# Cross attention whose transposed scores are computed a second time, with the maxima in a contraction row

## The chip, the cores and the metric

The kernel runs on one core of one Trainium2 chip. The metric is the device time of one execution in microseconds (us), lower is better. It is a decoder layer with batch 8, 112 tokens per batch and width 256: self attention, cross attention over 375 context tokens, and an expert layer, each followed by a layer norm. All arithmetic is float32.

## The reference, cut to what matters

Only the cross attention is touched. It has 16 heads of 16 columns each. In this case the scale is 1/4, and the mask has one row pattern for all batches and heads.

```python
q = _split_heads(query @ Wq.T + bq)      # (8, 16, 112, 16)
k = _split_heads(key @ Wk.T + bk)        # (8, 16, 375, 16)
v = _split_heads(value @ Wv.T + bv)
scale = 1.0 / jnp.sqrt(jnp.float32(HEAD_DIM))
scores = jnp.einsum('bhqd,bhkd->bhqk', q, k) * scale
scores = jnp.where(mask == 0, NEG_INF, scores)
probs = jax.nn.softmax(scores, axis=-1)
out = jnp.einsum('bhqk,bhkd->bhqd', probs, v)
out = out.transpose(0, 2, 1, 3).reshape(query.shape[0], -1, D_MODEL)
return out @ Wo.T + bo
```

## The kernel before, in words

Every engine has its own hand-written list of instructions, and semaphores join them. Nothing is scheduled by a tool: an instruction that waits holds back all that stands behind it on its engine.

**Slots.** Cross attention runs in 32 slots (`SLOTS`), n = 0 to 31. A slot handles four heads of one batch: b = n // 4 is the batch, g = n % 4 the group of heads. The four heads of a slot lie in four strips of 32 partitions (`STRIPS`), since a head has 16 columns and two heads share a strip; queries of the other head of the strip are zeroed in `qz`, so a contraction over 32 rows gives one head's scores.

**One slot before.** TensorE (PE) computes the scores of four heads, queries as weights (`score2`, L617), each 112x375 into its own PSUM bank. VectorE (DVE) reads each, adds the mask, writes the sum to `p2` and keeps its row extreme in `nm2` (`mask_and_max`, L1232; signs are turned, so the maximum is a minimum). ScalarE (ACT) takes the exponential from `p2` with that extreme as its bias (`exps2`, L996). PE transposes each 112x375 block of probabilities in three pieces of 125 columns (`turn2_`, L635, 12 transposes in a slot), and ACT (three heads, `evac_pt`, L1003) and DVE (one head, `evac_pt2`, L1240) copy the result from PSUM to `pT2`. PE multiplies with the values (`value2`, L651); a column of ones in `v2` gives the softmax sums.

**What stands between.** PE's list for slot n is: `score2(n)`, two transposes groups of slot n-1, a filler, the other two groups, more fillers, `value2(n-2)`. The fillers are the projections of the next batch's keys (`project_k`, L526) and values (`project_v`, L532), of queries for every second batch (`project_q`, L518), the transposes of the output (`turn_o`, `turn_on`), the output projection (`out2`, L670) and the transposes for the next layer (`turn_x2`). Keys go to SBUF on ACT (`evac_k`, L951), values with their bias on DVE (`evac_v`, L1181), the attention output of a batch on DVE (`evac_ot`, L1246), and DVE also does the division (`normalise2`), the second layer norm (`ln2_a`, `ln2_b`) and the query scaling (`evac_q`, L1174).

**Around it.** Self attention comes before, with its own loop over the 8 batches; DVE scales the queries' mask factor at the end of its batch 1 (`query_scale`), and `out1` (L504) is its output projection. After the slots PE runs the shared expert (`shared`, L790, `shared_down`, L801), while the router's decisions are made on DVE, GpSimd (POOL) scatters the tokens by indirect DMA (L384), and the sorted tiles are loaded back (L294) and transposed (`head_tile`, L848) for the loop over expert tiles.

## Time and profile before

| | |
|---|---|
| time, median of 3 runs | 438.22 us (438.16 to 438.72) |
| profiled execution | 438.09 us, its span 436.3 us |
| PE busy | 413.4 us, 95% of the span |
| DVE busy | 243.3 us, 56% |
| ACT busy | 193.8 us, 44% |
| POOL busy | 51.0 us, 12% |
| granted TensorE clock, mean | 0.996 of 2.4 GHz |

The span is what the profiler sees between the first and the last instruction; 1.8 us of the profiled execution lie around it. Busy shares are means over stages with different limits: self attention takes the first 165 us, the 32 slots lie between 164.7 and about 329 us, the shared expert and the routing up to 366 us, and the loop over expert tiles the rest. In the rows, PEld is the loading of weights, L617 a line of the kernel, and a bracket says how long the engine stood idle before the instruction and who released it.

### The profile page before, as it was taken

To read this page: it belongs to the slowest core of one execution; us is meant where nothing else is said; L and a number is where in the kernel's file an instruction comes from. 1 tells how busy PE (TensorE), PEld (TensorE's weight loads), DVE (VectorE), ACT (ScalarE), POOL (GpSimd) and SP (SyncE) were. 2 spreads that over 40 slices of the span, in tenths; PEclk is the share of its full clock that TensorE was granted. 3 is DMA by queue.
4 is the path that set the end of the run, shared out by engine and by line. 5 is a ranking of instruction groups with operands and counts; after the bars stand their busy time and mean duration, and the time that the engine had idled before them with its cause. 6 is when DMAs were issued, how large, how long until landed. Compare 5 with 4: busy or idle time off the path is not lost.

```text
span 436.3 us, 8960 instructions
## 1 busy us (share of the span) xinstructions
PE 413.4 (95%) x3125; PEld 296.9 (68%) x3126; DVE 243.3 (56%) x724; ACT 193.8 (44%) x580; POOL 51.0 (12%) x77
## 2 busy tenths in 40 slices
PE   8999999999999988999999999999989998999992
PEld 7767879778796765766776676767665474656661
DVE  1275765747556546666665676767762552244442
ACT  1164363343625536677666666767663101111110
POOL 4010010110101001000010101010100045212222
PEclk9999999999999999999999999999999999999998
DMA  8998000000000014040404131900000013122211
GB/s 248 373 382 236 19 2 2 0 2 2 1 2 0 2 37 145 2 181 16 167 16 167 52 131 46 390 37 2 2 2 2 1 50 108 49 62 69 62 42 33
DMA packets 15242, 34.22 MB, mean 78 GB/s; under 512 B 2382, under 2 KB 9151, under 8 KB 13921
## 3 DMA queue, kind: packets, MB, share of 16 engines
q1 hardware_dynamic: 13952, 30.70, 20.3%
q0 software_dynamic: 1104, 2.76, 1.8%
q8 instruction: 25, 0.41, 0.4%
q10 hardware_dynamic: 144, 0.23, 0.2%
q14 instruction: 17, 0.13, 0.1%
HBM read 27.24 MB, written 6.70 MB: 78 GB/s over the span
## 4 chain that ended last, share of the span: by engine, by line
PE 68%; issue 23%; DVE 4%; ACT 1%; SPq 1%; DMA 0%; POOLq 0%; POOL 0%; DVEq 0%; ACTq 0%
PE bank L434 11%; PE bank L635 7%; PE bank L448 7%; PE bank L504 6%; PE bank L617 4%; PE bank L880 4%; PE bank L856 4%; PE bank L532 3%; PE bank L862 3%; PE bank L465 3%; PE bank L491 3%; PE bank L526 3%; PE bank L651 3%; PE bank L477 3%; PE bank L801 1%
## 5 line engine op out<-in xcount | busy, mean ns | idle before, releaser
L1232 DVE CUSTOM_DVE_ANT_0 p<-bank,mask 112x375 f32<-112x375 f32 x128 | 62.7, 546 | 39.2 <-PE bank L617 39.2
L996 ACT ACTIVATE p<-p,nm 112x375 f32<-112x375 f32 x128 | 74.8, 609 | 5.9 <-DVE nm L1232 5.9
L635 PEld LDWEIGHTS bank<-ident,p 112*125 112x125 f32 x384 | 48.9, 187 | 22.8 <-issue 13.7
L1003 ACT ACTIVATE pT<-bank 125x336 f32<-125x336 f32 x96 | 42.9, 447 | 46.0 <-PE bank L635 46.0
L635 PE MATMUL bank<-ident,p 112*125 112x112 f32 x384 | 58.8, 286 | 0.9
L434 PE MATMUL bank<-x2T,arena 128*128 128x224 f32 x256 | 53.9, 359 | 0.0
L939 ACT ACTIVATE p<-bank,nm 112x112 f32<-112x112 f32 x128 | 43.6, 366 | 18.3 <-DVE nm L1106 18.3
L434 PEld LDWEIGHTS bank<-x2T,arena 128*128 128x128 f32 x256 | 47.3, 193 | 0.7 <-DMA x2T<-in_xT 0.6
L349 POOL TENSOR_TENSOR rstd<-veps,minus_half 128x1 f32<-128x1 f32 x14 | 7.7, 549 | 292.6 <-DVE veps L1132 292.6
L1106 DVE TENSOR_REDUCE nm<-bank 112x4 f32<-112x448 f32 x32 | 19.2, 620 | 24.1 <-PE bank L465 24.1
L1099 DVE TENSOR_SCALAR arena<-bank 128x448 f32<-128x448 f32 x32 | 19.9, 623 | 22.0 <-PE bank L434 22.0
L617 PE MATMUL bank<-kT,qz 32*112 32x375 f32 x256 | 28.8, 517 | 3.5 <-ACT x2T L965 2.1
L448 PE MATMUL bank<-arena,x2T 128*112 128x512 f32 x64 | 30.2, 602 | 0.0
L945 ACT ACTIVATE arena<-bank 128x448 f32<-128x448 f32 x16 | 8.7, 544 | 46.8 <-PE bank L491 46.8
L939 ACT ACTIVATION_READ_ACCUMULATOR p<-bank,nm 112x1 f32 x128 | 28.1, 220 | 0.0
L504 PE MATMUL bank<-arena 128*128 128x256 f32 x112 | 26.0, 385 | 1.4 <-ACT arena L945 1.0
L532 PE MATMUL bank<-wx,mid 128*125 128x256 f32 x96 | 26.5, 399 | 0.0
L790 PE MATMUL bank<-x2T,ugs 128*128 128x512 f32 (+1 forms) x64 | 25.5, 543 | 0.6 <-DVE pT L1313 0.4
L651 PE MATMUL bank<-pT,v 125*32 125x112 f32 x768 | 25.0, 263 | 0.0
L1073 ACT ACTIVATE p<-bank 128x512 f32<-128x512 f32 x9 | 5.4, 597 | 44.0 <-PE bank L856 44.0
L651 PEld LDWEIGHTS bank<-pT,v 125*32 125x32 f32 x768 | 17.3, 109 | 10.1 <-issue 7.4
L504 PEld LDWEIGHTS bank<-arena 128*128 128x128 f32 x112 | 20.7, 190 | 4.8 <-ACT arena L945 1.3
(140 smaller groups left out, 596.2 us busy)
## 6 DMA issues: line engine op xcount, KB each, us to landing
arena<-in_ug SPq DMA_DIRECT2D x8, 1024.0 KB, 5.8
arena<-in_dn SPq DMA_DIRECT2D x8, 512.0 KB, 6.7
mid<-in_ctxT SPq DMA_DIRECT2D x8, 375.0 KB, 3.1
slots_s<-blank SPq DMA_DIRECT2D x14, 128.5 KB, 3.6
arena<-in_wqk SPq DMA_DIRECT2D x7, 256.0 KB, 5.7
slots_x<-blank SPq DMA_DIRECT2D x14, 128.0 KB, 6.6
p<-slots_s SPq DMA_DIRECT2D x9, 128.5 KB, 2.0
kT<-slots_x SPq DMA_DIRECT2D x9, 128.0 KB
```

The costliest lines, as they stand in the source:

```text
L434: mm = pe.matmul(J[:, m * S_PAIR:(m + 1) * S_PAIR], wqk[:, 2 * u + m, k, :], xT[:, i, k, :], start=(k == 0), stop=(k == KC - 1))
L448: mm = pe.matmul(PE_J1[c][0:S, :], xT[:, b // 2, k, (b % 2) * S:(b % 2 + 1) * S], wv1[:, c, k, :], start=(k == 0), stop=(k == KC - 1))
L504: mm = pe.matmul(PE_W1[:, 0:C], oT1[:, k, t * TILE:(t + 1) * TILE], wout[:, k, :], start=(k == 0), stop=(k == 7))
L532: mm = pe.matmul(M[0:SK, 0:C], ctxT[:, b % 2, k, t * SK:(t + 1) * SK], wx[:, 2, k, :], start=(k == 0), stop=(k == KC - 1))
L617: mm = pe.matmul(PE_S2[r][0:S, 0:S2], qz[rows_r, b // 2 % 2, m, par, b % 2, :], kT2[rows_r, b % 2, m, :], start=True, stop=True)
L635: mm = pe.transpose(PE_T2[r][0:SK, t * S:(t + 1) * S], p2[i % RING][:, t * SK:(t + 1) * SK], ident[0:S, 0:S])
L651: mm = pe.matmul(PE_V2[VP * r:VP * r + VP, g * S:(g + 1) * S], v2[:, b % 2, t, g * STRIPS + r, :], pT2[0:SK, (n * STRIPS + r) % RING, t, : ...
L790: mm = pe.matmul(bank[2 + 2 * (n % 2) + part][:, 0:width(grp)], ugs[:, k, part * HID + m * 128:part * HID + (m + 1) * 128], x2T[:, k, grp ...
L939: e = act.activation(p1[g][:, n, :], PE_S1[g % 2][0:S, n * S:(n + 1) * S], ACT.Exp, bias=nm1[:, h:h + 1], accum_out=rs1[:, h:h + 1])
L996: act.activation(p2[i % RING], p2[i % RING], ACT.Exp, bias=nm2[:, i % H:i % H + 1], scale=-1.0).then_inc(exp2, 1)
L1003: act.activation(pT2[0:SK, i % RING], PE_T2[r][0:SK, 0:KT * S].rearrange("p (k n) -> p k n", k=KT), ACT.Copy).then_inc(pt2_act, 1)
L1232: v.tensor_tensor_reduce(p2[i % RING], PE_S2[r][0:S, 0:S2], bias[:], 1.0, 3e38, ALU.add, ALU.min, accum_out=nm2[:, i % H:i % H + 1]).then_ ...
```

## The change

The probabilities are no longer transposed. Instead the scores are computed a second time in transposed form, with the keys as weights, and the exponential is taken from that.

- A contraction of 32 rows has 16 rows that belong to the strip's other head, and they multiply zeros. `kx` now holds the keys twice, once for each parity of head, and in one of these rows (the pole) it holds -1. `mask_and_max` writes its extreme into the column of `nmx` that belongs to this row; PE transposes `nmx` (`turn_nm`), and DVE adds the transposed rows to the slot's queries (`add_nm`), which gives `qm`. The second product `kx` by `qm` (`score2_turned`) then is the score minus its maximum, already transposed: 3 pieces by 4 heads, each 125x112.
- ACT takes the exponential straight from PSUM to `pT2`, 125x336 for a head, with no bias.
- The mask isn't in the second product, so masked entries are set to zero after the exponential, with the transposed mask `maskT`: POOL does one head of a slot in two instructions (minimum with 1, then product), DVE three heads in one minimum over 125x1008 (`keep_unmasked`).
- Keys are written by ACT and DVE, half of the columns each, twice (for each parity). The value bias is folded into the output bias `rows[:, 1]` by a product in self attention's batch 1, and values and attention outputs are now copied by ACT (`evac_v2`, `evac_o2`).
- PSUM is shared differently: banks 0 to 3 hold the scores, banks 4 to 7 the transposed ones, and fillers borrow from both, so each waits for the mask or the exponential that frees its bank.
- `out1` of the last tile moves into slot 0, the projection of keys for batch 1 into self attention's last batch, `turn_x1(2)` out of it. Three pieces of the shared expert, in place of one, stand before the router's last transposes. `kx` lies over the weights of expert 0, so its load waits for the last `score2_turned`.

The core of the diff:

```diff
+        kx = arena[:, 0:4 * KC * S2].rearrange("p (b m a n) -> p b m a n", b=2, m=KC, a=2)
@@ sync
+            for j, e in enumerate(range(1, E)):
+                load_expert(e)
+                if j + 3 < B:
+                    load_ctx(j + 3)
+            sp.wait_ge(turned2, SLOTS)
+            load_expert(0)
@@ gpsimd
+            def keep_unmasked(n):
+                i = n * STRIPS
+                g.wait_ge(exp2, i + 1)
+                p = pT2[0:SK, i % RING].rearrange("p k n -> p (k n)")
+                g.tensor_scalar(p, p, 1.0, None, ALU.min).then_inc(at_most_one, 1)
+                g.wait_ge(at_most_one, n + 1)
+                g.tensor_tensor(p, p, maskT[0:SK, :], ALU.mult).then_inc(kept_pool, 1)
@@ tensor
+                    for k in range(KC):
+                        mm = pe.matmul(PE_W1[:, C:2 * C], bvw[:, k, :], wx[:, 3, k, :], start=(k == 0), stop=(k == KC - 1))
+                    mm.then_inc(bo_more, 1)
...
-            def turn2_(n, r):
-                for t in range(KT):
-                    mm = pe.transpose(PE_T2[r][0:SK, t * S:(t + 1) * S], p2[i % RING][:, t * SK:(t + 1) * SK], ident[0:S, 0:S])
+            def turn_nm(n):
+                pe.wait_ge(max2, (n + 1) * STRIPS)
+                pe.transpose(PE_N2, nmx[:, n % GROUPS, :], ident[0:S, 0:S]).then_inc(nm_pe, 1)
+            def score2_turned(n):
+                pe.wait_ge(qm_sb, n + 1)
+                lent_banks_back(n)
...
+                    pe.wait_ge(exp2, n * STRIPS)
+                for t in range(KT):
+                    for r in range(STRIPS):
+                        rows_r = slice(32 * r, 32 * r + 32)
+                        mm = pe.matmul(PE_T2[r][0:SK, t * S:(t + 1) * S], kx[rows_r, b % 2, m, par, t * SK:(t + 1) * SK],
+                                       qm[rows_r, n % 2, :], start=True, stop=True)
+            def fillers(n):
+                first_free(n)
...
+                elif g < 2 and b + 1 < B:
+                    pe.wait_ge(max2, n * STRIPS + 2)
+                    project_k(g, b + 1, [(PE_S2[0], 0, KH), (PE_S2[1], KH, S2)])
...
+                turn_nm(n)
...
+            for n in range(SLOTS):
+                score2(n)
+                if n >= 1:
+                    score2_turned(n - 1)
+                if n >= 2:
+                    value2(n - 2)
+                fillers(n)
@@ scalar
+            for n in range(SLOTS):
+                if n >= 1:
+                    exps2(n - 1, 0)
+                if n >= 2:
+                    evac_o2(n - 2)
+                if n >= 1:
+                    exps2(n - 1, 1)
+                first_out(n)
+                if n >= 1:
+                    exps2(n - 1, 2)
+                    exps2(n - 1, 3)
+                lent_out(n)
@@ vector
+            def keep_unmasked(n):
+                i = n * STRIPS + 1
+                v.wait_ge(exp2, i + 3)
+                p = pT2[0:SK, i % RING:i % RING + 3].rearrange("p r k n -> p r (k n)")
+                v.tensor_tensor(p, p, maskT[0:SK, :].unsqueeze(1).to_broadcast([SK, 3, KT * S]), ALU.min).then_inc(kept_dve, 1)
+            for n in range(SLOTS):
+                b, g = n // GROUPS, n % GROUPS
+                for r in range(STRIPS):
+                    mask_and_max(n, r)
+                if g < 2 and 1 <= b < B - 1:
+                    evac_k(g, b + 1, PE_S2[1])
+                if g == 2 and b >= 1:
+                    normalise2(b - 1, PE_A2)
+                add_nm(n)
+                if g == 3 and b >= 2:
+                    ln2_y(b - 2, PE_B2)
+                if n >= 1:
+                    keep_unmasked(n - 1)
+                if g == 3 and b >= 2:
+                    ln2_a(b - 2)
+                if g == 1 and b >= 3:
+                    ln2_b(b - 3)
+                if g == 2 and b in (0, 2, 4):
+                    evac_q(b // 2 + 1, PE_Q2)
```

How the order moves, for a slot in which keys of the next batch are projected. On DVE before, the second half of such a slot and the first pass of the next were (p<-bank,mask is `mask_and_max`, L1240 the copy of one transposed head, L1181 the values, L1262 `ln2_b`):

```order
336 L1232 ISA p,nm<-bank,mask 112x375 [waits scores2,turn2]
337 L1232 ISA nm 112x1
338 L1240 COPY pT<-bank 125x336 [waits pv2,turn2]
339 L1181 TENSOR_TENSOR v<-bank,rows 125x16x16 [waits v_pe]
340 L1262 TENSOR_SCALAR xres<-ybuf,mv,rstd 128x256 [waits rstd2]
341 L1232 ISA p,nm<-bank,mask 112x375 [waits scores2,turn2]
```

The same place on DVE now (L1273 is `evac_k`, L1363 `add_nm`, L1370 `keep_unmasked`):

```order
277 L1356 ISA p,nmx<-banks,mask 112x375 [waits scores2,max2]
278 L1356 ISA nmx 112x1
279 L1273 TENSOR_SCALAR arena<-banks,kscale,kbias 128x187 [waits k_pe]
280 L1273 TENSOR_SCALAR arena<-banks,kscale,kbias 128x187
281 L1363 TENSOR_TENSOR qm<-banks,qz 128x112 [waits nm_pe]
282 L1370 TENSOR_TENSOR pT<-pT,maskT 125x1008 [waits exp2]
283 L1356 ISA p,nmx<-banks,mask 112x375 [waits scores2,max2]
```

Between two slots' mask passes DVE now waits for the key projection, for the transposed extremes and for the last exponential of the slot before. On ACT before, such a slot was (L951 is `evac_k`, L1003 `evac_pt`, L996 `exps2`):

```order
171 L1003 ACTIVATE pT<-bank 125x336 [waits pv2,turn2]
172 L996 ACTIVATE p<-p,nm 112x375 [waits max2]
173 L1003 ACTIVATE pT<-bank 125x336 [waits pv2,turn2]
174 L996 ACTIVATE p<-p,nm 112x375 [waits max2] x2
```

And now on ACT (L1064 is `exps2`, L1079 `evac_o2`, L1014 `evac_k`):

```order
153 L1064 ACTIVATE pT<-banks 125x336 [waits pv2,turned2]
154 L1079 ACTIVATE oT<-banks 128x112 [waits pv2]
155 L1064 ACTIVATE pT<-banks 125x336 [waits pv2,turned2]
156 L1014 ACTIVATE arena<-banks,kbias,kscale 128x188 [waits k_consts,k_pe]
157 L1014 ACTIVATE arena<-banks,kbias,kscale 128x188
158 L1064 ACTIVATE pT<-banks 125x336 [waits pv2,turned2] x3
```

The two key copies stand between the second and the third exponential of the slot before (the third of the rows at 158 is already the first exponential of the next slot).

## Rows read from the trace of the kernel before

**Rows 1.** Stretches: start:end and length, busy of PE, PEld, DVE, ACT, POOL, clock, DMA

```profile
167.93:320.03 152.10, 147.71 (x1530) 105.53 (x1531) 101.34 (x347) 103.82 (x239) 8.26 (x13) 1.00 0.25 93
...
223.48:244.15 20.67, 20.08 (x212) 14.23 (x208) 13.62 (x48) 14.00 (x32) 1.25 (x2) 1.00 0.26 95
...
244.15:265.94 21.79, 21.66 (x220) 15.65 (x216) 14.75 (x50) 14.00 (x32) 1.25 (x2) 1.00 0.26 92
...
320.03:341.89 21.86, 20.05 (x152) 11.26 (x153) 7.90 (x25) 9.31 (x20) 1.35 (x3) 1.00 0.00 1
...
430.00:436.30 6.30, 0.00 (x0) 0.00 (x0) 0.94 (x4) 0.00 (x0) 2.07 (x3) 0.73 0.05 15
```

**Rows 2.** Timeline of slot 20: start, us, engine, line, operation, idle before

```profile
265.94 0.90 PE L617 MATMUL bank<-kT,qz 32*112 32x375 f32 x8
...
266.77 2.05 PE L635 MATMUL bank<-ident,p 112*125 112x112 f32 x12
...
267.10 0.55 DVE L1232 CUSTOM_DVE_ANT_0 p<-bank,mask 112x375 f32<-112x375 f32 x1 [0.34 <-PE bank L617]
...
267.57 0.54 DVE L1232 CUSTOM_DVE_ANT_0 p<-bank,mask 112x375 f32<-112x375 f32 x1
...
268.51 0.54 DVE L1232 CUSTOM_DVE_ANT_0 p<-bank,mask 112x375 f32<-112x375 f32 x1
...
268.65 1.12 PE L532 MATMUL bank<-wx,mid 128*125 128x256 f32 x4
...
269.40 1.04 PEld L526 LDWEIGHTS bank<-mid,wx 128*128 128x128 f32 x4
...
270.96 0.54 PEld L651 LDWEIGHTS bank<-pT,v 125*32 125x32 f32 x24 [0.53 <-issue]
...
271.07 0.57 ACT L951 ACTIVATE kT<-bank,cols 128x375 f32<-128x375 f32 x1 [0.57 <-PE bank L526]
...
271.68 0.29 PEld L617 LDWEIGHTS bank<-kT,qz 32*112 32x112 f32 x8 [0.17 <-issue]
```

**Rows 3.** Timeline at the end of slot 0: last mask pass, next scores

```profile
167.26 0.55 DVE L1232 CUSTOM_DVE_ANT_0 p<-bank,mask 112x375 f32<-112x375 f32 x1
...
167.93 0.32 PEld L617 LDWEIGHTS bank<-kT,qz 32*112 32x112 f32 x8 [1.46 <-DVE nm L1232]
```

**Rows 4.** Costliest groups of the page: copies of one transposed head

```profile
L996 ACT ACTIVATE p<-p,nm 112x375 f32<-112x375 f32 x128 | 74.8, 609 | 5.9 <-DVE nm L1232 5.9
...
L1003 ACT ACTIVATE pT<-bank 125x336 f32<-125x336 f32 x96 | 42.9, 447 | 46.0 <-PE bank L635 46.0
```

**Rows 5.** Timeline: two ACT copies back to back, and one DVE copy

```profile
326.02 0.79 ACT L1003 ACTIVATE pT<-bank 125x336 f32<-125x336 f32 x2 [1.18 <-PE bank L635]
...
328.47 0.51 DVE L1240 COPY pT<-bank 125x336 f32<-125x336 f32 x1 [1.17 <-PE bank L635]
```

**Rows 6.** Line L1114, a DVE product from SBUF: ns min/median/max

```profile
L1114 DVE TENSOR_TENSOR p<-p,rc x32: 624/624/627, 24.4 to 155.1; 112x448 f32<-112x448 f32 x32
```

**Rows 7.** Line L354, a POOL sum: ns min/median/max

```profile
L354 POOL TENSOR_TENSOR xb<-xres,rows x7: 722/738/1151, 27.5 to 134.4; 128x256 f32<-128x256 f32 x7
```

**Rows 8.** Timeline of DVE when the longest of the L354 sums ran

```profile
27.42 0.62 DVE L1114 TENSOR_TENSOR p<-p,rc 112x448 f32<-112x448 f32 x1
```

**Rows 9.** Timeline: weight loads of self attention's scores, two strips

```profile
144.49 0.86 PEld L465 LDWEIGHTS bank<-arena 64*112 64x112 f32 x16
```

**Rows 10.** Timeline of DVE: first and last step of the second layer norm's statistics

```profile
265.34 0.42 DVE L1125 TENSOR_TENSOR ybuf<-bank,xb 128x256 f32<-128x256 f32 x1 [0.44 <-PE bank L670]
...
266.60 0.15 DVE L1132 TENSOR_SCALAR veps<-mv 128x1 f32<-128x1 f32 x1
```

**Rows 11.** Timeline: output projection in batch 2, and the last one

```profile
54.42 3.69 PE L504 MATMUL bank<-arena 128*128 128x256 f32 x16 [0.34 <-DVE qscale L1162]
...
161.06 3.72 PE L504 MATMUL bank<-arena 128*128 128x256 f32 x16 [1.05 <-ACT arena L945]
```

**Rows 12.** Timeline: the first sorted tile's transposes

```profile
366.03 0.44 PE L848 MATMUL bank<-ident,kT 128*128 128x128 f32 x2 [0.88 <-DMA kT<-slots_x]
```

More of the change, by code:

```diff
@@ L366, in add_bo, with root_and_next @@
                     g.wait_ge(y2, t - 1)
-                g.tensor_tensor(xb[:, t % 2], xres[:, t], rows[:, 2], ALU.add).then_inc(xb2, 1)
+                g.tensor_tensor(xb[:, t % 2], xres[:, t], rows[:, 1], ALU.add).then_inc(xb2, 1)
+            g.wait_ge(bo_sum, 1)
             add_bo(0)
             add_bo(1)
-            for t in range(NT):
+            def keep_unmasked(n):
[5 more added lines that the diff above has]
+                g.tensor_tensor(p, p, maskT[0:SK, :], ALU.mult).then_inc(kept_pool, 1)
+            def root_and_next(t):
                 g.wait_ge(ve2, t + 1)
@@ L375, in _ @@
                     add_bo(t + 2)
+            g.wait_ge(maskt_sb, 1)
+            for n in range(SLOTS):
+                if n == SLOTS - 1:
+                    root_and_next(NT - 2)
+                keep_unmasked(n)
+                if n % GROUPS == 3 and 2 <= n // GROUPS < B - 1:
+                    root_and_next(n // GROUPS - 2)
+            root_and_next(NT - 1)
             g.wait_ge(q_sb, PAIRS)
@@ L805, in _ @@
             pe.wait_ge(w_loaded["shared"], 32)
+            logits_t(0, 4, bank[0])
+            score2_turned(SLOTS - 1)
+            value2(SLOTS - 2)
+            shared(0, 0)
+            shared(0, 1)
+            turn_x2(NT - 2, bank[1])
             value2(SLOTS - 1)
-            logits_t(0, 4, bank[0])
-            pe.wait_ge(y2, NT - 1)
-            turn_o(B - 1)
             logits_t(4, 2, bank[1])
-            turn_on(B - 1)
-            shared(0, 0)
-            out2(NT - 1)
-            shared(0, 1)
+            turn_o(B - 1, PE_M2)
             shared(1, 0)
+            turn_on(B - 1, PE_M2)
+            shared(1, 1)
+            out2(NT - 1, PE_M2)
+            shared(2, 0)
+            shared(2, 1)
             pe.wait_ge(y2, NT)
             turn_x2(NT - 1, PE_M2)
-            shared(1, 1)
             logits_t(NT - 1, 1, bank[7])
@@ L946, in evac_o, with evac_k, evac_x1 @@
                                PE_U1[half][:, 0:4 * S].rearrange("p (k n) -> p k n", k=4), ACT.Copy).then_inc(ot1[half], 1)
-            def evac_k(m, b, J=PE_M2):
+            def evac_k(m, b, J):
                 act.wait_ge(k_pe, b * KC + (m + 1))
-                act.activation(kT2[:, b % 2, m, :], J[:, 0:S2], ACT.Identity, bias=cols[:, 1, m:m + 1]).then_inc(k_sb, 1)
-            def evac_x1(t, M=PE_M2):
+                act.wait_ge(k_consts, 3)
+                for par in range(2):
+                    last = act.activation(kx[:, b % 2, m, par, 0:KH], J[:, 0:KH], ACT.Identity, bias=kbias[:, m, par:par + 1],
+                                          scale=kscale[:, par:par + 1])
+                last.then_inc(k_act, 1)
+            def evac_x1(t, M):
                 act.wait_ge(x1t_pe, t + 1)
@@ L1059, in _ @@
             evac_logits(1, 0, 4, bank[0])
-            evac_on(B - 1)
+            evac_x2(NT - 2, bank[1])
+            evac_o2(SLOTS - 1)
+            shared_silu(0)
+            evac_on(B - 1, PE_M2)
             evac_logits(2, 4, NT - 1, bank[1])
-            shared_silu(0)
+            shared_silu(1)
             evac_x2(NT - 1, PE_M2)
-            for n in range(1, 2 * HT):
+            for n in range(2, 2 * HT):
                 shared_silu(n)
@@ L1155, in query_scale @@
             def query_scale():
+                v.wait_ge(w_loaded["small"], 16 * 10)
+                v.tensor_copy(bvw, cols[:, 2, :].unsqueeze(2).to_broadcast([128, KC, 128])).then_inc(bv_wide, 1)
+                v.wait_ge(bo_more, 1)
+                v.tensor_tensor(rows[:, 1], PE_W1[:, C:2 * C], rows[:, 1], ALU.add).then_inc(bo_sum, 1)
+                v.tensor_scalar(keep, bias[:], 0.0, None, ALU.is_equal).then_inc(keep_sb, 1)
                 v.wait_ge(q_any, 1)
@@ L1206, in _ @@
                     evac_qk(9 + 4 * b)
+                if b == B - 2:
+                    evac_k(1, 0, PE_J1[1], KH)
                 if b == B - 1:
-                    evac_q(0, PE_J1[1])
+                    evac_q(0, [PE_J1[1][:, m * S_PAIR:(m + 1) * S_PAIR] for m in range(KC)])
                 evac_pt(2, b)
@@ L1302, in _ @@
-            ln2_a(NT - 2)
-            ln2_b(NT - 2)
-            evac_pt2(SLOTS - 1)
-            evac_ot(B - 1)
-            normalise2(B - 1)
-            ln2_a(NT - 1)
-            ln2_b(NT - 1)
+                if g < 2 and 1 <= b < B - 1:
+                    evac_k(g, b + 1, PE_S2[1])
+                if g == 2 and b >= 1:
+                    normalise2(b - 1, PE_A2)
+                add_nm(n)
+                if g == 3 and b >= 2:
+                    ln2_y(b - 2, PE_B2)
+                if n >= 1:
+                    keep_unmasked(n - 1)
@@ L1313, in shared_product @@
                 v.tensor_tensor(hTs[:, k % HT, 0:width(k // HT)], gs[:, 0:width(k // HT)], bank[3 + 2 * (k % 2)][:, 0:width(k // HT)], ALU.mult).then_inc(sh_h, 1)
+            shared_product(0)
+            ln2_y(NT - 1, PE_M2)
+            ln2_a(NT - 1)
+            shared_product(1)
+            ln2_b(NT - 1)
             n = [0]
```

514 lines of the change are left out of this document (260 added, 254 removed).

## The prediction, made before the changed kernel had run

> **What bounds the kernel now.** I read the page's shares first, then the stretches of the 32 slots, then the timeline of one slot, and last the waits of DVE and ACT in it. The slots from the second to the last take 152.10 us, in which PE is busy 147.7, DVE 101.3 and ACT 103.8 [rows 1]. A batch of four slots takes 20.67 (three such), and 21.79 where queries are projected (two such) [rows 1]. In slot 20 the reader sees PE go from one group to the next with no gap of its own: scores 0.83, two turns, values' projection 0.75, keys' projection, `value2` 0.72, and the next scores [rows 2]. DVE waits 0.34 for scores, ACT 0.57 for keys. So the slots are bound by PE's list, and DVE has a third of its time free. The clock is 1.00 in these stretches.
>
> **What the change takes from PE.** Out go 12 transposes a slot: 266.77 to 268.65, 1.88 us, of which some is waiting, since six of them alone load in about 0.65; I count 1.3 as work. In come 24 small passes of `score2_turned`. Four strips run side by side in `score2` (8 passes of 375 columns end in 0.90), and `value2` has the same 24 passes of 112 columns and holds PE for 0.72 (270.96 to 271.68) [rows 2]. I take 0.71. The upper bound is weight loads that don't overlap: with two strips 16 loads of 112 columns took 0.86, 0.054 each, so 24 take 1.3 and the group 1.4 [rows 9]. The lower is 0.56, the passes alone at 0.0233 each. `turn_nm` adds 0.12. PE thus loses 1.3 - 0.83 = 0.47 us of work in a slot.
>
> **What it puts on DVE.** Per slot out goes a copy of 0.51 [rows 5], of which 0.41 is the pitch. In comes `add_nm`, 112 elements, 0.27 (pitch 0.18), and `keep_unmasked`, 1008 elements. Length: 448 elements take 0.624 and 256 take 0.42 [rows 6, 10], so 1.04 ns each and 0.157 fixed, and back to back an operation starts 0.09 before the last has ended. That gives 1.21, pitch 1.12. Keys add twice 0.26 in half the slots; the value copies (0.42, three a batch) and `evac_ot` leave. The sum for DVE in a batch is 16.8 of about 21 us: still under PE's, so by busy time nothing would stand in the way. A page's rule could have halved the 1.12: the Trainium skill, "VectorE: DVE Perf Modes", section "Why tensor_tensor can't do 2×_2P or 4×", says that an operation on two tensors has no port left to fetch two elements, so float32 keeps one per cycle. Row L1114 agrees, with both inputs in SBUF and the same rate.
>
> **Where the new waits close a loop.** DVE's list is mask passes of n, key copies, `add_nm(n)`, `keep(n-1)`, mask passes of n+1. In a slot with a key projection (g = 0, 1):
> - the second mask pass starts 0.47 after the first, and PE goes on 0.67 after its start [rows 2, 3]: 1.14
> - PE projects the keys; ACT starts on them 269.40 to 271.07 = 1.67 after the first load [rows 2]; the last pass has only 187 columns, so I take 1.60, and 0.05 for a start: 2.79
> - ACT copies keys twice; a pair of 336-element copies takes 0.79, so the pitch is 0.35 and 188 elements with a bias about 0.33: 0.66 [rows 5]: 3.45
> - exponentials r = 2 and 3 of slot n-1, 0.35 of pitch and 0.45 of length [rows 4, 5], and 0.05: 4.30
> - `keep(n-1)`, 1.12: 5.42, and the next slot's first mask pass starts.
>
> The exponential is priced as the copy of the same size. With a bias and from SBUF it took 0.609 for 375 elements [rows 4]; at that rate 0.09 more each.
>
> The slot g = 1 also has `ln2_b`, 0.32: 5.73. In g = 2 DVE waits for PE: last mask pass at 1.41, 0.67 to PE, `turn_nm` 0.12, values 0.82, `turn_on` 0.25, and 1.21 from scores to the mask pass (265.94 to 267.10 is 1.16 [rows 2]): 4.48. In g = 3: 1.41 + 0.67 + 0.12, then `out2` and its latency 1.2 and 0.05, `ln2_y` 0.33, `keep` 1.12, `ln2_a` 1.10 (with `ln2_y` 265.34 to 266.75 = 1.41 [rows 10]): 6.00. A batch is 5.42 + 5.73 + 4.48 + 6.00 = 21.6, against 20.67. The query batches: 1.5 more on PE and 1.2 on DVE, 1.95 in all, 23.3 and 23.6 against 21.8. Batch 1 has no layer norm yet, 19.9; the three slots of batch 0 come to 15.2 and the last three to 12.7. The sum is 15.2 + 19.9 + 23.3 + 3 x 21.6 + 23.6 + 12.7 = 159.5: **7.4 us more than 152.10.** Waits followed the same way from the same rows give 152.0 for the kernel before, so I trust it to a few us. POOL's pair is hidden: 336 elements at the rate of L354 are about 0.97 [rows 7] and the minimum about 0.76, 1.8 together, beside a slot of over 4; it becomes a bound only at twice that.
>
> **Stage before.** In self attention's batch 1 PE has 4 more passes of 256 columns (0.85) and DVE two more operations (0.33 + 0.45) ahead of the query factor, for which `out1` waited already [rows 11]: +1.5. The mask's transposes +0.35, key copies in batch 6 +0.3. In batch 7 a projection (1.25) stands for transposes (0.25): +1.0; then the four key copies on ACT (1.4) stand ahead of the copy that `out1` waits for [rows 11]. Scores of slot 0 come 0.2 before the old time (3.7 of `out1` moved behind them), but slot 1 needs `add_nm(0)`, which stands behind the statistics of `out1`'s layer norm on DVE (1.4). The second slot's scores start at 170.8 in place of 167.93: **+2.9 us** (range 1.5 to 4).
>
> **Stage behind.** From the last scores to the router's last transposes it took 21.86 [rows 1]. Now: 11.3 to `value2(31)`, of which 10.3 is PE work, and 12.1 from there, with an `out2` to `turn_x2` wait of 0.6 no longer covered, +1.5. DVE has one product of 0.69 fewer in the routing chain, -0.65. PE arrives 3.4 earlier at the first sorted tile, where it waits for the DMA already [rows 12]; it only waits longer. **+0.9 us** (range -1.5 to 3). Expert 0's 1.5 MB load starts about 6 us behind slot 31 and is needed some 40 later.
>
> **Sum.** 438.09 + 2.9 + 7.4 + 0.9 = 449.3 for the profiled execution, which lies 0.13 under the median of the runs: **449.4 us**, 2.5% slower.
>
> **Rivals.**
> - *TensorE stays the bound and the slots shrink with its work.* For it: 95% busy. Then 30 to 31 slots save 0.47 each, 14.5: 438.1 - 14.5 + 3.8 = 427.4 us. It decides from where a batch takes 20.67 - 4 x 0.47 = 18.8, so the two loops of 5.4 and 5.7 would have to close in about 4.7. Against it: every step of the loop is a wait in the lists, at a length that a row shows. Chance 0.15.
> - *The loop closes, but `keep` costs half*, as with two elements a cycle. Then the loop turns by 0.53 less, the slots take 149.7: 438.1 - 2.4 + 3.8 = 439.5 us. Rows L1114 and the page above speak against it. Chance 0.06.
> - *Weight loads of 125 columns don't overlap* [rows 9]: group 1.4, slots 166.7, 0.7 more at the end: 457.3 us. `score2`'s 8 loads in 0.29 (the last row of [rows 2]) speak against it. Chance 0.12.
> - *DVE and POOL block each other.* The longest L354 sum took 1.151 in place of 0.738, and it began while L1114, with two SBUF inputs, ran [rows 7, 8]. If POOL's pair starts first in the slots, `keep` is held for up to 0.97, 6 to 10 us over all: 457 us. In my list POOL starts 0.7 or more behind the end of `keep`, so it decides only where DVE is late. The Trainium skill, "SBUF — State Buffer", section "SBUF: two separate sides", has the pair of ports as an exclusive lock, held for the whole instruction, against a DVE operation with two SBUF inputs; by that rule the trace's 1.151 is a wait, and the kernel would move to this rival's time. Chance 0.07. A longer idle time of PE ahead of the sorted tiles (3.6 us) could also cost clock: at the end, after PE's last work, the mean granted is 0.73 [rows 1]. I give that 1 to 2 us inside the ranges.
>
> **Numbers.** The forecast's own case, 442 to 455, has 0.60. A difference of 0.2% (0.9 us) is about what a measurement can tell from none. Slower: 0.60 + 0.12 + 0.07 and a third of the 0.06, 0.81. Faster: 0.15 and a little, 0.16. Same: 0.03. The range runs from 439, which takes in the half-cost case, to 459, which takes in both slow rivals; the fast rival is what it leaves out.
>
> **What would show it.** `keep`, 125x1008, near 1.21 us, and its wait named after the exponential in the slots with keys; starts of the scores 5.4 apart there; a batch near 21.6 and the stretch of 31 slots near 159.5; `score2_turned` in about 0.7; PE's busy share in the slots well down, and its waits on DVE. Scores of slot 1 at 170.8. I am wrong if the stretch is under 149, if a DVE step is far from its row, or if PE is still busy for 97% of the slots.

## The result and the profile after

The changed kernel takes 454.49 us in the median of four runs (453.54 to 459.27), the kernel before 438.19. The ratio is 1.040, with a 95% interval of 1.037 to 1.043: the change makes it slower. The forecast was 449.4 us, with a range of 439 to 459. The profiled execution took 453.93 us, its span 452.2, so 15.8 us more than the one before, where 11.2 were forecast. The longest of the four, 459.27 us, had a mean granted TensorE clock of 0.982 of 2.4 GHz, the others 0.989 to 0.994; the kernel before has 0.996.

Where the 15.8 us lie can be read from when the scores of slots 1 and 31 start, and the router's last transposes: 174.33, 333.94 and 357.18 us now, against 167.93, 320.03 and 341.89 [rows 1]. That is 6.4 us ahead of slot 1, 7.5 in the 30 slots up to the last scores, 1.4 up to the router, and 0.6 from there to the end.

The same stretches as in [rows 1], of the kernel after (start:end and length, busy of PE, PEld, DVE, ACT, POOL, clock, DMA share, GB/s):

```profile
174.33:333.94 159.61, 130.18 (x1968) 96.15 (x1969) 124.65 (x370) 74.81 (x208) 66.08 (x73) 1.00 0.22 82
276.88:298.41 21.53, 17.87 (x270) 13.09 (x269) 16.94 (x52) 10.56 (x29) 9.00 (x10) 1.00 0.43 167
253.28:276.88 23.60, 19.43 (x278) 14.69 (x277) 18.10 (x54) 10.56 (x29) 9.00 (x10) 1.00 0.23 85
333.94:357.18 23.24, 21.76 (x187) 11.72 (x186) 10.88 (x26) 9.15 (x22) 5.28 (x7) 1.00 0.19 69
```

PE was busy for 147.7 of 152.1 us and is now for 130.2 of 159.6: the change did take 17.5 us of work from it, and the slots still became longer. DVE went from 101 to 125. No engine is busy for more than 82% of the slots, so it is an order of waits that sets them. The timeline of a slot with a key projection (start, us, engine, line, operation, idle before):

```profile
283.06 0.90 PE L677 MATMUL banks<-arena,qz 32*112 32x375 f32 x8 [0.24 <-DVE qm L1363]
...
283.51 1.21 DVE L1370 TENSOR_TENSOR pT<-pT,maskT 125x1008 f32<-125x1008 f32 x1 [0.59 <-ACT pT L1064]
283.85 0.92 PE L702 MATMUL banks<-qm,arena 32*125 32x112 f32 x24
284.63 0.54 DVE L1356 CUSTOM_DVE_ANT_0 p<-banks,mask 112x375 f32<-112x375 f32 x1
...
285.80 1.51 PE L572 MATMUL banks<-mid,wx 128*128 128x188 f32 x8 [0.20 <-DVE nmx L1356]
...
287.35 0.91 ACT L1014 ACTIVATE arena<-banks,kbias,kscale 128x188 f32<-128x188 f32 x2 [1.08 <-PE banks L572]
287.35 0.85 DVE L1273 TENSOR_SCALAR arena<-banks,kscale,kbias 128x187 f32<-128x187 f32 x2 [0.76 <-PE banks L572]
288.12 0.27 DVE L1363 TENSOR_TENSOR qm<-banks,qz 128x112 f32<-128x112 f32 x1
288.15 0.79 ACT L1064 ACTIVATE pT<-banks 125x336 f32<-125x336 f32 x2
288.53 0.90 PE L677 MATMUL banks<-arena,qz 32*112 32x375 f32 x8 [1.12 <-DVE qm L1363]
288.97 1.21 DVE L1370 TENSOR_TENSOR pT<-pT,maskT 125x1008 f32<-125x1008 f32 x1 [0.59 <-ACT pT L1064]
```

The reader can walk the loop here: `keep` (`keep_unmasked`, the minimum with the mask on DVE, L1370) at 283.51, mask pass 284.63, second pass, PE's key projection 285.80, ACT's key copies 287.35, its last two exponentials 288.15, `keep` again at 288.97. That is 5.46 us; 5.42 were forecast. At 289 `keep` waits 0.59 us for the exponentials. DVE's own list has little room beside it: `keep`, four mask passes, the key copies and the sum follow one another with only one more wait, of 0.76.

The biggest surprise is ahead of the slots. In self attention's batch 6, and at its end:

```profile
142.01 0.85 DVE L1273 TENSOR_SCALAR arena<-banks,kscale,kbias 128x187 f32<-128x187 f32 x2 [0.90 <-ACT arena L1014]
...
143.54 0.57 PE L519 MATMUL banks<-ident,p 112*112 112x112 f32 x4 [1.22 <-DVE pT L1197]
...
164.93 1.71 ACT L1014 ACTIVATE arena<-banks,kbias,kscale 128x188 f32<-128x188 f32 x4
165.94 1.65 DVE L1273 TENSOR_SCALAR arena<-banks,kscale,kbias 128x187 f32<-128x187 f32 x4 [3.03 <-ACT arena L1014]
...
168.00 0.90 PE L677 MATMUL banks<-arena,qz 32*112 32x375 f32 x8 [2.79 <-DVE arena L1273]
```

DVE's half of each key bank waits for ACT's half, and PE for DVE. In the code this is `if lo: v.wait_ge(k_act, ...)`: here both halves lie in one PSUM bank, and the kernel orders the two engines that read it. The Trainium skill, "PSUM — Partial Sum Buffer", section "PSUM bank collisions raise a hardware error", says why it must: no two engines may use a bank in the same partitions at once, not even to read; no run here shows what would follow. In the slots the halves lie in two banks, and the copies start together (287.35).

### The profile page after: what moved, and what is told of

It reads as the page before. It is cut to its first block, busy times and chain, and to the rows that moved or that the text cites. A ratio compares the mean times of both kernels' runs of the same rounds, so it can differ in the third digit from the quotient of the medians.

```text
span 452.2 us, 9961 instructions
## 1 busy us (share of the span) xinstructions
PE 397.8 (88%) x3596; PEld 288.4 (64%) x3597; DVE 274.6 (61%) x768; ACT 164.1 (36%) x553; POOL 113.1 (25%) x142
## 4 chain that ended last, share of the span: by engine, by line
PE 34%; DVE 15%; issue 7%; ACT 4%; POOL 1%; DMA 1%; DVEq 0%; POOLq 0%; ACTq 0%
DVE p L1356 6%; PE banks L848 4%; PE banks L572 4%; DVE pT L1370 4%; PE banks L941 4%; PE banks L917 3%; PE banks L923 3%; PE banks L583 3%; ACT pT L1064 2%; PE banks L702 2%; PE banks L717 1%; ACT arena L1014 1%; PE banks L736 1%; PE banks L677 1%; PE banks L859 1%
## 5 line engine op out<-in xcount | busy, mean ns | idle before, releaser
L1064 ACT ACTIVATE pT<-banks 125x336 f32<-125x336 f32 x128 | 52.7, 453 | 45.7 <-PE banks L702 45.6
L1356 DVE CUSTOM_DVE_ANT_0 p<-banks,mask 112x375 f32<-112x375 f32 x128 | 62.5, 545 | 5.9 <-PE banks L677 4.0
L400 POOL TENSOR_SCALAR pT<-pT 125x336 f32<-125x336 f32 x32 | 33.5, 1046 | 93.6 <-ACT pT L1064 93.6
L476 PE MATMUL banks<-x2T,arena 128*128 128x224 f32 x256 | 54.0, 359 | 0.0
L1000 ACT ACTIVATE p<-banks,nm 112x112 f32<-112x112 f32 x128 | 43.6, 366 | 20.3 <-DVE nm L1183 20.2
L476 PEld LDWEIGHTS banks<-x2T,arena 128*128 128x128 f32 x256 | 47.3, 193 | 0.7 <-DMA x2T<-in_xT 0.5
L372 POOL TENSOR_TENSOR rstd<-veps,minus_half 128x1 f32<-128x1 f32 x14 | 7.8, 560 | 153.3 <-DVE veps L1209 140.3
L1370 DVE TENSOR_TENSOR pT<-pT,maskT 125x1008 f32<-125x1008 f32 x32 | 40.1, 1253 | 10.0 <-ACT pT L1064 10.0
L677 PE MATMUL banks<-arena,qz 32*112 32x375 f32 x256 | 28.8, 517 | 14.2 <-DVE qm L1363 10.3
L490 PE MATMUL banks<-arena,x2T 128*112 128x512 f32 x64 | 30.2, 602 | 0.0
L402 POOL TENSOR_TENSOR pT<-pT,maskT 125x336 f32<-125x336 f32 x32 | 28.7, 896 | 2.7
```

Source lines behind the costliest of these rows:

```text
L400: g.tensor_scalar(p, p, 1.0, None, ALU.min).then_inc(at_most_one, 1)
L476: mm = pe.matmul(J[:, m * S_PAIR:(m + 1) * S_PAIR], wqk[:, 2 * u + m, k, :], xT[:, i, k, :], start=(k == 0), stop=(k == KC - 1))
L490: mm = pe.matmul(PE_J1[c][0:S, :], xT[:, b // 2, k, (b % 2) * S:(b % 2 + 1) * S], wv1[:, c, k, :], start=(k == 0), stop=(k == KC - 1))
L677: mm = pe.matmul(PE_S2[r][0:S, 0:S2], qz[rows_r, b // 2 % 2, m, par, b % 2, :], kx[rows_r, b % 2, m, par, :], start=True, stop=True)
L1000: e = act.activation(p1[g][:, n, :], PE_S1[g % 2][0:S, n * S:(n + 1) * S], ACT.Exp, bias=nm1[:, h:h + 1], accum_out=rs1[:, h:h + 1])
L1064: act.activation(pT2[0:SK, i % RING], PE_T2[r][0:SK, 0:KT * S].rearrange("p (k n) -> p k n", k=KT), ACT.Exp, scale=-1.0).then_inc(exp2, 1)
```

## Experiments

Times are medians. The ratio in each is to the kernel before, run beside it on the same chip, with its 95% interval.

**1. Less work for PE.** The values' products run over one of three key tiles; the two others' are left out.

```diff
-                for t in range(KT):
+                for t in (KT - 1,):
...
```

> The value products of cross attention run over the last of the three key tiles alone; those of the first two are left out (8 of 12 passes of a slot). TensorE loses 0.76 x 2/3 = 0.5 us of busy time in each of 32 slots, some 16 us. Theory A (a circle through VectorE sets the slots: mask passes, turned maxima, products, exponentials, minimum on VectorE) expects 1 us less, since these passes stand beside VectorE's work: the stretch from the scores of slot 1 to those of slot 31 stays at 158.5 to 159.5 us (159.75 now), the whole at 452 to 454 us. Theory B (TensorE's work still bounds the slots) expects 10 to 15 us less, 440 to 444 us.

Measured: 456.22 us, 1.040 (1.037 to 1.044), not faster at all. The timeline of PE in the same kind of slot:

```profile
285.61 0.90 PE L677 MATMUL banks<-arena,qz 32*112 32x375 f32 x8 [0.24 <-DVE qm L1363]
...
287.37 0.40 PE L717 MATMUL banks<-pT,v 125*32 125x112 f32 x8
...
288.34 1.51 PE L572 MATMUL banks<-mid,wx 128*128 128x188 f32 x8 [0.58 <-DVE nmx L1356]
...
291.07 0.58 PE L677 MATMUL banks<-arena,qz 32*112 32x375 f32 x4 [1.12 <-DVE qm L1363]
```

The products fell from 0.78 to 0.40, PE's wait ahead of the projection grew from 0.20 to 0.58, and the slot is 5.46 again. PE does not bound it. Theory A stands and B falls. It isn't quite nothing: in the 23 slots away from any stretch at half clock (1 to 11 and 16 to 27) PE lost 8.7 us of work and they took 122.2 us in place of 123.9, 1.7 less, most of it in slots 3, 11 and 19, which stand behind a projection of queries. The whole stretch of slots is 161.0 us, longer than the expected 159, for a reason that neither theory had: PE's clock. The stretches of this run, with the columns as above (the clock stands behind POOL):

```profile
177.62:338.64 161.02, 124.70 (x1505) 87.96 (x1505) 124.82 (x370) 73.30 (x208) 65.91 (x73) 0.97 0.22 81
325.00:331.00 6.00, 4.22 (x41) 2.82 (x45) 3.72 (x11) 1.07 (x3) 2.75 (x4) 0.72 0.00 0
```

The granted clock is 0.97 over the slots, with whole microseconds at half (1.2 GHz of 2.4 GHz) in it. In the four runs the mean was 0.974 to 0.985, in the kernel before 0.995 to 0.997.

**2. Less work for DVE.** The minimum with the mask covers one of DVE's three heads; the mask of the two others is left out.

```diff
-                p = pT2[0:SK, i % RING:i % RING + 3].rearrange("p r k n -> p r (k n)")
+                p = pT2[0:SK, i % RING + 2:i % RING + 3].rearrange("p r k n -> p r (k n)")
...
```

> VectorE's minimum with the mask covers 336 columns, one of its three heads; the mask of the two others is left out. VectorE loses 672 columns, 0.70 us in each of 32 slots (22 us of its busy time). Theory A (circle through VectorE) expects the stretch of slots at 148 to 151 us (159.75 now, worked out from the rows' durations), where TensorE's 130 us of busy time with its waits take over, and the whole at 442 to 446 us. Theory B (TensorE bounds) expects 454 us again, within 1 us.

Measured: 444.64 us, 1.017 (1.015 to 1.020). Its slots, from the scores of slot 1 to those of slot 31:

```profile
175.18:324.36 149.18, 128.81 (x1969) 95.71 (x1969) 106.10 (x370) 74.72 (x208) 66.07 (x73) 1.00 0.23 88
```

The slots fell from 159.6 to 149.2 us, as theory A had it. Taking 0.38 us of each slot from PE had given next to nothing, and taking 0.6 from DVE (18.5 in all) gives 10.4 us. This is the main proof that `keep` on DVE is a link of the loop that turned the saving into a loss: with it cut down the slots are shorter than the 152.1 of before. It is not the only link, as the next experiment shows.

**3. ACT's order.** Key copies behind the exponentials.

```diff
-                elif g < 2 and b + 1 < B:
-                    evac_k(g, b + 1, PE_A2)
...
                     exps2(n - 1, 3)
+                if 1 <= n // GROUPS < B - 1 and n % GROUPS < 2:
+                    evac_k(n % GROUPS, n // GROUPS + 1, PE_A2)
```

> Only the order on ScalarE changes: in the 12 slots of batches 1 to 6 with a key projection, its two key copies (0.91 us) come behind the four exponentials of the slot, not between the second and the third. Theory A says that the third and fourth exponential then end 0.9 us earlier, VectorE's minimum begins 0.9 us earlier, and the circle of these slots is shorter by 0.5 to 0.7 us: 6 to 8 us less for the stretch (152 to 154 us), 446 to 449 us for the whole. Theory B expects no change, or up to 1 us more, since the next scores wait for keys that are copied later.

Measured: 449.24 us, 1.029 (1.026 to 1.033), the slots 153.45 us. No work was removed, only a wait: the idle time ahead of `keep` fell from 8.5 to 1.5 us (its row among the groups of the slots, mean ns and then idle time):

```profile
L1370 DVE TENSOR_TENSOR pT<-pT,maskT 125x1008 f32<-125x1008 f32 x30 | 38.2, 1274 | 1.5 <-ACT pT L1064 1.5
```

The second key slot of a batch takes 5.04 us in place of 5.46, the slot behind it 4.53 in place of 5.22. So the loop ran through ACT's copies, as the forecast's sum has it. The whole lies just above the 446 to 449 us expected.

**4. One engine to a bank.** In self attention DVE copies the whole bank of one half of the channels, ACT that of the other.

```diff
-                if lo:
-                    v.wait_ge(k_act, b * KC + (m + 1))
+                first = 0 if b < 2 else KH
...
```

> In self attention (batches 6 and 7) the four key banks are no longer shared out in halves between two engines: VectorE copies the whole bank of one half of the channels and ScalarE that of the other, two copies of 375 columns each, so VectorE's key copies wait for no copy of ScalarE. Theory C (the 3.5 us that the stage before the slots took beyond the forecast are VectorE standing behind ScalarE at the shared bank) expects the first scores of slot 1 2.5 to 3.5 us earlier than 174.3 us and the whole at 451 to 452 us. Rival D (the time went into the length of the copies themselves, 375 columns times two parities instead of one plain copy) expects less than 1 us, since the same columns are copied.

Measured: 454.30 us, 1.036 (1.033 to 1.039). Slot 1's scores start at 171.38 in place of 174.33, 2.95 us earlier, so theory C is right and D wrong. Of these, 0.25 us stood already ahead of batch 1 (its scores at 36.52 and 36.77), so the edit gives 2.7. Batch 6 loses 1.3 us of its 2.05 us of delay; its timeline has DVE's copies without a wait, and PE waits 0.62 us where it was 1.22:

```profile
140.78 1.24 DVE L1276 TENSOR_SCALAR arena<-banks,kscale,kbias 128x375 f32<-128x375 f32 x2
...
142.70 0.57 PE L519 MATMUL banks<-ident,p 112*112 112x112 f32 x4 [0.62 <-DVE pT L1201]
```

But the whole hardly moved: four of the six runs had a granted clock of 0.981 or 0.982 and took 454.0 to 455.3 us, the two at 0.993 took 450.6 and 451.9. The profiled one has three half-clock stretches in its slots, where the changed kernel's has none, and its slots take 162.4 us, 2.8 more. So in this run the clock took back what the edit gave.

**5. DVE and POOL.** POOL's product with the mask is left out; the clamp stays.

> GpSimd clamps the first head to 1 as now and leaves out its product with the mask (0.90 us a slot). If VectorE's minimum waits while GpSimd's product runs (its longest took 1.60 us, one that began while the product ran, against 1.20 us alone), its mean falls from 1.24 to 1.20 to 1.21 us, the idle time ahead of it shrinks a little, and the slots become 1 to 1.5 us shorter. If the two do not get in each other's way, the durations stay at a mean of 1.24 us and the whole is the same within 0.5 us. Theory B (TensorE bounds the slots) expects nothing either way.

`keep`'s row among the groups of the slots:

```profile
L1368 DVE TENSOR_TENSOR pT<-pT,maskT 125x1008 f32<-125x1008 f32 x30 | 36.1, 1203 | 8.6 <-ACT pT L1062 8.5
```

Its mean fell from 1.243 to 1.203 us, but the idle time ahead of it did not shrink (8.5 and 8.6 us) and the slots gave only 0.3 us (159.3). POOL does hold DVE up: in the changed kernel the `keep` of 343.41 started 0.36 us into a product of POOL (343.05, 0.90 long) and took 1.60. Five of the 32 started in a product or sum of POOL's and took 1.30 to 1.62, four of them in the 30 slots, and none in the loop of the middle slots. It is worth 0.3 us here, against 1 to 1.5 expected. The whole was 459.13 us, 1.049 (1.047 to 1.051), and says nothing on this: other probabilities route the tokens otherwise, and the loop over sorted tiles ran once more (from the first sorted tile to the end 78.0 us in place of 71.9).

**6. The wait for the first sorted tile.** A shared pass ahead of its transposes.

```diff
-            head_tile(0, True)
-            e = gates_ups(0)
             shared(7, 0)
+            head_tile(0, True)
+            e = gates_ups(0)
```

> Behind the router the first of the last two shared passes (1.33 us) is put ahead of the transposes of the first sorted tile, so that TensorE has work while the sorted rows come from memory (2.13 us of waiting now). Theory: the wait costs twice in the changed kernel, by its own length and because a stretch at half clock follows it (granted clock 0.84 from 382 to 392 us, six passes of L848 in 3.52 us where before eight took 2.84 us). If so, 1.3 us is won by the pass and another 1 to 1.6 us by the clock: 451 to 452 us where 454 stood. Rival: the half clock comes whatever stands in the wait, and only 0.8 to 1.3 us is won.

Measured: 453.56 us, 1.034 (1.032 to 1.037). From the first sorted tile to the end it takes 69.2 us, the changed kernel 71.9. PE's timeline in the changed kernel, and then its clock in one stretch of it:

```profile
380.33 0.44 PE L909 MATMUL banks<-ident,spent 128*128 128x128 f32 x2 [2.13 <-DMA spent<-slots_x]
380.99 4.53 PE L848 MATMUL banks<-x2T,ugs 128*128 128x384 f32 x8 [0.22 <-issue]
```

The stretch behind the wait:

```profile
382.00:386.00 4.00, 4.00 (x8) 2.09 (x8) 0.37 (x1) 0.49 (x1) 0.00 (x0) 0.61 0.20 62
```

Eight passes took 4.53 us, most of it at half clock, where the kernel before needs 2.84 (its wait was 0.88 [rows 12]). With the wait filled (0.84 us are left of it) the clock stays at 1.00 and 2.7 us are won in this stretch. How much of it is the clock can be read from experiment 2's kernel, whose wait was not filled and whose clock did not fall:

```profile
370.86 0.44 PE L909 MATMUL banks<-ident,spent 128*128 128x128 f32 x2 [2.26 <-DMA spent<-slots_x]
371.52 2.84 PE L848 MATMUL banks<-x2T,ugs 128*128 128x384 f32 x8 [0.22 <-issue]
```

From there to its end it took 70.2 us: 1.7 of the 2.7 are the clock, 1.0 the wait. So such a wait does not always bring the half clock. Of the seven profiled kernels with this wait unfilled (2.0 to 2.4 us) six had half clock behind it, of the five with it filled none.

The whole gained less than the 451 to 452 us expected: the profiled run lost 1.7 us in slot 0 (8.01 for 6.32) and 1.8 in the slots behind, at half clock both times. The one run of the five with a clock of 0.997 took 451.02 us.

**7. Four changes of order together** (experiments 3, 4, 6, and the query factors first in batch 1).

```diff
-                v.wait_ge(bo_more, 1)
-                v.tensor_tensor(rows[:, 1], PE_W1[:, C:2 * C], rows[:, 1], ALU.add).then_inc(bo_sum, 1)
-                v.tensor_scalar(keep, bias[:], 0.0, None, ALU.is_equal).then_inc(keep_sb, 1)
                 v.wait_ge(q_any, 1)
...
```

These lines come back later: the comparison behind the query factors of batch 1, the sum in batch 2.

> The four changes of order together: key copies of ScalarE behind the exponentials, one engine for each key bank in self attention, query factors ahead of the bias work in batch 1, a shared pass in the wait for the first sorted tile. If they add up: 454.2 less 6.2, 2.9, 1.3 and 2.5 us, 441 to 442 us, still 3 to 4 us above the kernel before (438 us); the stretch of slots 153.5 us. If the circle through VectorE is the same resource in all, the sum would stop short at 445 us or more. Should TensorE's clock fall more often in the slots, as it did with the bank rule alone (granted clock 0.981 in four of six runs), 1 to 1.5 us is added for each stretch.

Measured: 443.17 us, 1.012 (1.010 to 1.014), 1 to 2 us more than expected; slot 1 at 171.45 and the slots 154.9, with one half-clock stretch (its slot, slot 30, took 5.65 us, the same one in experiment 3 4.52). The factor gave less than expected, which a run of that edit alone shows too.

> The query factors first in batch 1, bias product in batch 2 and mask transposes in batch 3, alone, everything else as in the changed kernel. In the run with four orders the groups of batch 3 on stood 0.46 us earlier (relative to the start of the second batch's scores), since 1.06 and 0.52 us of TensorE work came back in batches 2 and 3. Expected here: the same 0.4 to 0.5 us at the scores of batch 3 and of slot 0.

Measured, one run: 458.05 us at a clock of 0.982. Counted from the scores of batch 1, the second score group of batch 2 starts 1.53 us earlier than in the changed kernel, batch 3's first 0.98, and from batch 4 to slot 0 it is 0.46. So the wait went, and 1.07 us of it came back as PE's own work in batches 2 and 3 (the bias product takes 1.04, the transposes 0.58). From 60 to 90 us PE has no wait there that they could fill, so they are paid.

**8. More order.** So the bias product goes to a wait of PE's (ahead of slot 0), the statistics of slot 0 behind `add_nm`, and in the key slots the projection starts in halves.

> Beside the four changes of order: in the 12 slots with a key projection its first half of the columns starts behind the first mask pass, its second behind the second, and the value products of the slot come behind it (in spare columns of another bank, whose copy by ScalarE comes last); the bias product (1.06 us of TensorE in a stretch that TensorE bounds) stands in the wait ahead of the first scores; the layer norm statistics of slot 0 (1.33 us of VectorE) stand behind the sum of maxima and queries. Theory A (VectorE's circle in the key slots, whose copies waited 0.72 us for the projection): 0.3 us less in each of 12 slots, 150 to 151 us for the stretch of slots (153.8 without its one half-clock stretch), slot 1 at 169.2 to 169.8 us (171.45), the whole 437 to 439 us where 443.2 stood, level with the kernel before. Rival: the later value products (0.6 us) hold up the products of the next slot, and the stretch stays at 153.5 us or more.

> The same with 250 of the 375 key columns copied by ScalarE and 125 by VectorE (188 and 187 before) in batches 2 to 7. VectorE's two copies become 0.13 us shorter and ScalarE's 0.12 us longer in each of 12 slots. Theory A expects 1 to 1.6 us less than six_orders, since VectorE's circle is what counts and ScalarE stands idle half of the time; the rival (ScalarE's copies, now behind the exponentials, end last and hold the next scores) expects the same time or up to 1.5 us more.

Measured: 440.04 us, 1.005 (1.004 to 1.007), and 439.53 us, 1.005 (1.003 to 1.006). Slot 1 is at 168.42. That is better than the 169.2 to 169.8 expected, but the whole misses its 437 to 439 by 1 us. The slots take 153.3, with a half-clock stretch in them (150 to 151 were expected); the second slot of a batch fell from 5.04 to 4.72 us, the first is at 6.25 (6.18 before), where the value products now end late (the rival, in half the slots). The division of the key columns makes no difference: theory A expected 1 to 1.6 us and is wrong on it. The trace with 250 columns shows why:

```profile
271.60 0.28 DVE L1385 TENSOR_TENSOR qm<-banks,qz 128x112 f32<-128x112 f32 x1 [0.23 <-PE banks L693]
```

DVE's two copies take 0.72 us in place of 0.85, and then DVE waits 0.23 us for PE's transposed extremes (`turn_nm`, L693), which stand behind the value products. The sum starts at 271.60, and at 271.62 in the kernel with 187 columns.

> As six_orders, but in the first slot of each of batches 1 to 6 the value products stand again ahead of the key projection, where TensorE waits 1.28 us for the second mask pass (they then took 0.78 us behind it and pushed the value projection and the next scores back: the slot stayed at 6.25 us while the second slot of a batch fell from 5.03 to 4.71 us). Theory A: this slot falls by 0.4 to 0.6 us, six times, so the stretch of slots 150 to 151 us (152.2 in six_orders without its half-clock stretch), the whole 436.5 to 438 us, level with or just under the kernel before. Rival: VectorE's own work in that slot (minimum, statistics, four mask passes, copies, sum) fills it, and the slot stays at 6.2 us: 440 us again.

Measured: 437.65 us (12 runs), 0.999 (0.997 to 1.001): level with the kernel before. The first slot of a batch takes 5.70 where it took 6.25, as theory A had it. The stretch of slots is 152.0 with two half-clock stretches in it, the first of them in the second row:

```profile
168.64:320.64 152.00, 132.74 (x1969) 98.79 (x1969) 126.30 (x374) 74.68 (x208) 67.09 (x73) 0.98 0.23 87
172.00:177.00 5.00, 4.67 (x63) 3.58 (x64) 3.67 (x11) 1.22 (x5) 3.20 (x3) 0.66 0.27 107
```

Its three runs with a clock of 0.996 took 435.9 to 436.3 us, those at 0.984 439.1 and 439.2. The clock is worth 3 us between the ends.

**9. The kernel before, with experiment 6's edit.**

> The kernel before the change, with the one edit of order that has nothing to do with the change: the shared pass (1.33 us) ahead of the transposes of the first sorted tile, where its TensorE waits 0.88 us. If the 2.7 us that this gave the changed kernel between the first sorted tile and the end came from the wait and from the half clock behind it, the kernel before can win no more than its shorter wait, since it has no half clock there: 0.4 to 0.9 us, 437.2 to 437.7 us. The rival: the half clock is not behind that wait and the pass itself is worth 2 us anywhere: 435.5 to 436.5 us.

Measured: 438.77 us, 1.002 (1.001 to 1.004): 0.8 us slower, outside both expectations. The pass is longer than the wait that it fills, and the first gate passes then waited 1.72 us for the copy of the transposes. So the edit is no gain in itself; it repaired a longer wait that only the changed kernel has. The other edits of order concern lists that only the changed kernel has, and were not tried on the kernel before.

## Why the prediction was right, and where it was off

*What bounds the slots.* Right, and shown from both sides: less work for PE gives 1.7 us of 8.7 (experiment 1), less for DVE 10.4 us of 18.5 (2), and ACT's copies lie in the loop (3). The step's size was right too: 159.5 forecast, 159.6 measured. It holds slot by slot, if one counts as the forecast does, from the first mask pass of a slot to that of the next: the four slots of batch 5 take 5.42, 5.78, 4.48 and 5.85 us, forecast were 5.42, 5.73, 4.48 and 6.00. A batch takes 21.53 (21.6 forecast), one with queries 23.60 (23.6). `keep` takes 1.208 us in the median, 1.21 forecast.

Single terms were off. Round the loop of 283.51 to 288.97 two of them cancelled: PE's projection and the start of the copies took 1.55 us (1.65 forecast), ACT's two key copies 0.80 (0.66). `score2_turned` holds PE for 0.75 to 1.06 us until the next group, some of it waiting, between the 0.71 chosen and the rival's 1.4 and nearer the first. DVE's key copies have a pitch of 0.39 (the time from one start to the next), not 0.26, and hide behind ACT's; POOL's minimum took 1.05, not 0.76, and is hidden.

*The stage before.* This step failed in its size: +2.9 us forecast (1.5 to 4), +6.4 measured, outside the step's own range. The whole of the miss lies ahead of the slots: the scores of slot 0 were to start 0.2 us earlier than before and start 3.3 later (168.00 against 164.71), while slot 0 itself, forecast at 6.3 us, took 6.32. The sum had "key copies in batch 6 +0.3" and then "four key copies on ACT (1.4)". Batch 6 cost 2.05 us, since DVE's copies stood behind ACT's at the shared bank; at the end of batch 7 the same wait set the first scores (2.79 us of PE's idle time). The forecast took the copies of the two engines as work side by side and overlooked one `wait_ge` in the code. Experiment 4 gives back 2.7 us of the 3.5 that were missed; the other 0.8 is not traced. Batch 1 was near: 2.08 us with the mask's transposes, 1.85 forecast.

*The stage behind.* 0.9 forecast, 1.9 measured. Up to the router +1.4 (1.5 forecast). From there to the first sorted tile 1.0 less (0.65 forecast), and then 1.5 more, behind a stretch at half clock. The forecast had named such a loss ("1 to 2 us inside the ranges") and left it out of the sum; the wait that it tied it to is 2.13 us, not 3.6.

*The total.* 449.4 against 454.49: 3.5 us of the miss are the stage before, 0.1 the slots, 1.0 the stage behind. The rest is that the median lies 0.56 us above the profiled run and not 0.13; in two of the other runs the granted clock was lower (0.982 and 0.989 against 0.994).

*The rivals.* PE as the bound: refuted by 1. `keep` at half cost: 1.208 us measured. Weight loads that don't overlap: 24 passes hold PE for 1.06 us at most, not 1.4, and the slots stayed at 159.6, not 166.7. DVE and POOL: the effect is there (five of 32 `keep` took 1.30 to 1.62 us), and worth 0.3 us. The Trainium skill, "SBUF — State Buffer", section "SBUF: two separate sides", has the port pair as a lock that the engine that starts first holds for its whole instruction. The five agree but for 0.14 us, and as a rival it failed for the reason given, that POOL's product is seldom at work when `keep` starts. With the better orders it is more often: 11 of 32 in experiments 3 and 7, 2.5 us of DVE's time in all.

*What stays open.* That PE's idle time brings the half clock is argued from where it fell, not shown by an experiment that changes nothing else. Filling the sorted tile's wait (6) kept it up, but experiment 2's kernel kept it up too, with the wait unfilled. What else decides it is not known.

## What to carry to other kernels

Work taken from the busiest engine is worth what the next loop of waits allows. Walk the loop by its rows, engine by engine, before counting busy shares: here 17.5 us less for TensorE became 7.5 us more, because one VectorE operation of 1.2 us, with ScalarE's key copies in front of it, closed a ring. When an operation is shared out between two engines, look at where both halves are read from, and for the wait that orders them. And when such a change has gone wrong, the order of the other engines' lists is the first thing to try: with next to no work taken out, it gave back 16.8 us here (454.49 to 437.65). That is the level of the kernel before and no more: as it was tried here, the change never became a gain.

## What the runs showed of the hardware

- TensorE's clock falls to half for a few us more often once the engine waits in every slot. The kernel before shows a mean of 0.994 to 0.997 in its runs; the changed kernel and its variants 0.974 to 0.997, and it differs from run to run of one kernel. In the profiled runs of the changed kernel and its eleven variants PE has, between 100 and 400 us, 25 waits of 2.0 to 2.8 us: ahead of the scores of slot 0, near slot 28 and ahead of the first sorted tile. With or within 2 us of 17 of them the clock fell to half (4 of 7, 7 of 11, 6 of 7). Seven falls came elsewhere. The kernel before has no wait over 1.3 us there and no fall. One fall cost 1.1 to 1.7 us where it could be read (a slot of 5.65 for 4.52; eight passes of 4.53 for 2.84; slot 0 in 8.01 for 6.32). So a change can be right on work and waits and still be off by some us a run.
- A VectorE operation with two inputs in SBUF that starts while GpSimd works on a product or sum of two tensors is held. The one at 343.41 started with 0.54 us of GpSimd's left and took 1.60 us in place of 1.20, 0.39 more. In all profiled runs together, 71 of `keep` started with over 0.2 us left, and each was longer by what was left less 0.14 us. Three (at 172.1, 172.3 and 172.5 us in the kernels of experiment 8) started with 0.34 us left of GpSimd's minimum with a constant, which has one tensor input, and took 1.19 us: they were not held.
- VectorE's copy of 187 elements from PSUM with a scale and a bias per partition takes 0.47 us at a pitch of 0.39, and a comparison of 375 elements in SBUF against a constant took 0.35; at the rate of [rows 6] they would take 0.35 and 0.55. The first is longer, the second shorter.
